# A list of steps per engine in the attention stage, and a whitening without its bias row

## The reference, cut to what matters

```python
x = x + _L0_conv_ref(_ln_c(x), ...)          # windowed attention: 16 heads of 8 channels, windows of 64 tokens
t = t + _L0_ffn_ref(_ln_t(t), ...)           # MoE: softmax of the logits, best 2 of 8 experts, w2(silu(w1 t) * (w3 t))
x = x + _L1_conv_ref(_ln_c(x), gamma, beta)  # whitening in 4 groups of 32 channels
t = t + _L1_ffn_ref(_ln_t(t), ...)           # MoE with biases and a third matrix

def _L1_conv_ref(x, gamma, beta):
    f = jnp.transpose(x, (3, 0, 1, 2)).reshape(C, N)
    mean = jnp.mean(f, axis=1, keepdims=True)
    f = f - mean
    fg = f.reshape(g, m, N)
    cov = jnp.einsum('gmn,gkn->gmk', fg, fg) / (jnp.float32(N) - 1.0)
    ...                                       # sig = cov / trace, three Newton steps for P
    whiten = P / jnp.sqrt(tr)
    fhat = jnp.einsum('gmk,gkn->gmn', whiten, fg)
    return out * gamma + beta
```

## Time and profile before

| | before |
|---|---|
| median of three runs | 790.41 us (789.06 to 793.35) |
| the profiled execution | 785.86 us, span 784.1 us |
| TensorE (PE) busy | 574.4 us, 73% of the span |
| VectorE (DVE) busy | 449.5 us, 57% |
| ScalarE (ACT) busy | 344.2 us, 44% |
| GpSimd (POOL) busy | 424.3 us, 54% |

### The profile page before, as it was taken

The page is one execution under the profiler, slowest core; times in us unless marked ns, Lnnn a source line. Parts: engine busy times, 40 slices in busy tenths (PEclk is TensorE's granted clock), DMA queues, the critical chain, the costliest instruction groups (busy, mean ns, idle before and its releaser), DMA issues. The chain is left out here.

```text
span 784.1 us, 16744 instructions
## 1 busy us (share of the span) xinstructions
PE 574.4 (73%) x5440; PEld 417.1 (53%) x5440; DVE 449.5 (57%) x1248; ACT 344.2 (44%) x860; POOL 424.3 (54%) x417
## 2 busy tenths in 40 slices
PE   3777777876775774869989992997464386999950
PEld 1244454544553563758766671775353265888840
DVE  2675658597684774563434442945662646666635
ACT  2545464453624543656645561431402263555520
POOL 4454345365833464577774445512277774777760
PEclk9858798796966787989979996899866596999985
DMA  9999999999993002231443314200015272556418
GB/s 345 179 177 166 179 160 176 165 168 168 167 166 55 13 29 63 65 104 56 122 133 119 118 60 163 66 2 1 3 45 88 58 123 71 126 132 148 91 40 319
DMA packets 114996, 90.77 MB, mean 116 GB/s; under 512 B 9391, under 2 KB 104760, under 8 KB 114528
## 3 DMA queue, kind: packets, MB, share of 16 engines
q1 hardware_dynamic: 105840, 72.08, 48.8%
q0 software_dynamic: 8640, 16.93, 6.6%
q10 hardware_dynamic: 432, 0.68, 0.3%
HBM read 35.37 MB, written 55.20 MB: 116 GB/s over the span
## 5 line engine op out<-in xcount | busy, mean ns | idle before, releaser
L639 POOL DMA_INDIRECT results<-fetched,rowbuf x142 | 138.0, 972 | 69.9 <-issue 36.1
L940 DVE SCALAR_TENSOR_TENSOR work<-work,rowbuf,bank 128x256 f32<-128x256 f32 x142 | 68.0, 479 | 82.0 <-ACT work L764 67.6
L1314 PE MATMUL bank<-W,work 128*128 x568 | 92.3, 287 | 1.0 <-DVE fetched L947 0.5
L764 ACT ACTIVATE work<-bank 128x256 f32<-128x256 f32 x142 | 54.4, 383 | 78.3 <-PE bank L1301 76.5
L1299 PE MATMUL bank<-Wh,xl 128*128 x142 | 73.1, 515 | 9.6 <-DVE xl L931 6.4
L1314 PEld LDWEIGHTS bank<-W,work 128*128 128x128 f32 x568 | 78.4, 200 | 2.5 <-issue 1.4
L652 POOL DMA_INDIRECT region<-rows_a,where x64 | 63.3, 989 | 22.6 <-issue 19.8
L1306 PE MATMUL bank<-C,work 128*128 128x128 f32 x284 | 57.2, 285 | 17.7 <-DVE work L940 17.6
L1232 PE MATMUL bank<-PT,Vm 64*32 64x64 f32 x2048 | 44.2, 247 | 32.0 <-issue 19.7
L1232 PEld LDWEIGHTS bank<-PT,Vm 64*32 64x32 f32 x2048 | 38.5, 126 | 51.8 <-issue 46.4
L1306 PEld LDWEIGHTS bank<-C,work 128*128 128x128 f32 x284 | 39.9, 146 | 43.0 <-issue 17.4
(11 more groups left out here) (230 smaller groups left out, 1252.7 us busy)
## 6 DMA issues: line engine op xcount, KB each, us to landing
region<-pad SPq DMA_DIRECT2D x32, 1040.0 KB, 19.8
rowbuf<-region SPq DMA_DIRECT2D x142, 65.0 KB
fetched<-results SPq DMA_DIRECT2D x16, 512.0 KB, 4.5
spare<-w1gv_dram SPq DMA_DIRECT2D x8, 640.0 KB
spare<-b_dram SPq DMA_DIRECT2D x71, 64.0 KB
results<-fetched,rowbuf POOLq DMA_INDIRECT x142
work<-w_dram SPq DMA_DIRECT2D x8, 256.0 KB, 12.0
W<-w_dram SPq DMA_DIRECT2D x2, 1024.0 KB, 12.0
```

Of the source, the lines that this page charges most:

```text
L639: pool.indirect_dma_start(results[layer], bass.IndirectOffsetOnAxis(ap=at, axis=0), ysb[:, T % YRING, :], None, bounds_check=PAIRS - 1, oo ...
L764: act.activation(sg[:, i % 2, :], bank[:, b, 0:FF], ACT.Silu).then_inc(sg_sb, 1)
L940: v.scalar_tensor_tensor(out=hh[:, i % 2, :], in0=sg[:, i % 2, :], scalar=tile_rows(i)[:, GATE_AT:GATE_AT + 1], in1=bank[:, b, FF:2 * FF], ...
L1314: last = mm(bank[:, b, 0:P], hT[:, i % 2, ft * P:(ft + 1) * P], W2[layer][:, bass.ds(experts[i] * FT + ft, 1), :].rearrange("p a n -> p (a ...
```

## The change

**The lists.** `LAYER0` becomes a list per engine. A table SHIFT holds, for each engine and kind of step, a number that is added to the step's number before the sort. In `ORDER`, S now stands ahead of O. `MIDDLE` and `LAYER1` are sorted as before.

**The whitening.** `brow`, its product and its sum are gone. ScalarE subtracts the mean from the features (eight activations, which wait for VectorE's value of minus the mean, L1109). GpSimd adds beta to `X` in `MIDDLE`, four steps after a block's c_stats. TensorE waits for the matrix and for a block's centred features; ahead of block 0 it does no warm-up product any more.

```diff
-COV_STEP = {"pair": -1, "sum0": 0, "c_stats": 0, "yc": 1, "yturn": 2, "mean": 2, "cov": 3}
+COV_STEP = {"pair": -1, "sum0": 0, "c_stats": 0, "yc": 1, "yturn": 2, "mean": 2, "cov": 3, "beta": 4}
-ORDER = ("up", "Vm0", "Vm1", "O", "S", "J", "V0", "V1", "ht", "dn", "out", "xt",
+ORDER = ("up", "Vm0", "Vm1", "S", "O", "J", "V0", "V1", "ht", "dn", "out", "xt",
+SHIFT = {
+    "PE": {"T": 0.37, "turn": 0.14, "K": 0.63, "S": -0.35, "J": -0.28, "Q": 0.05, "PT": 0.01, "V1": 0.07, "logits": 0.03},
+    "ACT": {"split": -0.39, "PT": 0.11, "T": 0.44, "exp": 0.97, "turn": 0.27, "rows": 0.17, "Kb1": 0.15, "gates": 1.09, "Vm1": -0.65, "a_y": 0.06},
...
-def in_order(steps):
-    return [(name, i) for _, _, i, name in sorted((s, ORDER.index(name), i, name) for s, name, i in steps)]
+def in_order(steps, shift):
+    return [(name, i) for _, _, i, name in
+            sorted((round(s + shift.get(name, 0), 3), ORDER.index(name), i, name) for s, name, i in steps)]
-LAYER0, MIDDLE, LAYER1 = in_order(first_layer()), in_order(between()), in_order(second_layer())
+LAYER0 = {engine: in_order(first_layer(), SHIFT[engine]) for engine in SHIFT}
+MIDDLE, LAYER1 = in_order(between(), {}), in_order(second_layer(), {})
...
-            if name == "white":
-                if i == 0:
-                    pool.wait_ge(brow_sb, 1)
+            if name == "beta":
                 pool.wait_ge(y_sb["c"], BT * (i + 1))
-                pool.tensor_tensor(xb(i), xb(i), over_tiles(brow[:, :]), ALU.add).then_inc(x_beta, 1)
+                pool.tensor_tensor(xb(i), xb(i), over_tiles(par("beta")), ALU.add).then_inc(x_beta, 1)
...
+            act.wait_ge(newton, MEAN_STEP)
+            for i in range(BLOCKS):
+                wait_freed(act, "yturn", i)
+                act.activation(features(i), features(i), ACT.Identity, bias=minus_mean[:, 0:1]).then_inc(centred, 1)
...
-            dve.wait_ge(newton_ps, 3 * (NEWTON_STEPS - 1) + 4)
-            nc.vector.tensor_tensor(brow[:, :], bank[:, NEWTON1, 0:P], par("beta"), ALU.add).then_inc(brow_sb, 1)
...
                 if i == 0:
-                    pe.wait_ge(brow_sb, 1)
-                warm(b, WARM_BLOCK)
+                    pe.wait_ge(wh_ready, 2)
+                else:
+                    warm(b, WARM_BLOCK)
+                pe.wait_ge(centred, i + 1)
...
-            pe.wait_ge(wh_ready, 2)
-            mm(bank[:, NEWTON1, 0:P], minus_mean[:, 0:1].to_broadcast([P, P]), whiten, start=True, stop=True)\
-                .then_inc(newton_ps, 1)
```

More of the change, by code:

```diff
@@ L134 @@
         3: (18,) * 4 + (19,) * 4 + (20,) * 4 + (21,) * 4}
-ORDER = ("up", "Vm0", "Vm1", "O", "S", "J", "V0", "V1", "ht", "dn", "out", "xt",
+ORDER = ("up", "Vm0", "Vm1", "S", "O", "J", "V0", "V1", "ht", "dn", "out", "xt",
          "a_y", "Kb0", "Kb1", "rows", "route", "white", "max", "sub", "J_add", "stats1", "a_stats", "Q_turn", "K_turn", "sum", "exp",
          "Q0", "Q1", "norm", "yc", "pair", "sum0", "T", "turn", "logits", "gates", "place", "list", "put",
-         "PT", "Q", "K", "split", "fold_w", "fold", "c_stats", "cov", "yturn", "mean")
+         "PT", "Q", "K", "split", "fold_w", "fold", "c_stats", "beta", "cov", "yturn", "mean")
+SHIFT = {
+    "PE": {"T": 0.37, "turn": 0.14, "K": 0.63, "S": -0.35, "J": -0.28, "Q": 0.05, "PT": 0.01, "V1": 0.07, "logits": 0.03},
+    "ACT": {"split": -0.39, "PT": 0.11, "T": 0.44, "exp": 0.97, "turn": 0.27, "rows": 0.17, "Kb1": 0.15, "gates": 1.09, "Vm1": -0.65, "a_y": 0.06},
+    "DVE": {"a_stats": -1.65, "rows": -0.35, "a_y": -1.06, "list": 0.88, "Q_turn": -0.1, "place": 0.45, "max": -0.29, "sum": 0.21},
+    "POOL": {"split": 0.9, "T": 1.49, "route": 0.31, "Q0": -1.38, "K_turn": 0.52, "a_stats": -0.57, "put": -0.3, "Q1": -0.58},
+}
 def tile_steps(layer, at):
@@ L220, in bank_fills @@
     table, needs, filled, turn, pair_end, single_end = {}, {}, [0] * 8, {}, [0] * 8, [0] * 8
-    for name, i in LAYER0 + MIDDLE + LAYER1:
+    for name, i in LAYER0["PE"] + MIDDLE + LAYER1:
         if name in TURNS:
@@ L345, in build @@
         N2, whiten = covd, cov
-        brow = sb("brow", [P, P])
         rowbuf2 = sb("rowbuf2", [P, RING // 2, ROW])
@@ L399, in build @@
         mean_row, means_set = sem("mean_row"), sem("means_set")
-        newton, newton_ps, centre_d, wh_ready, brow_sb = (sem(n) for n in (
-            "newton", "newton_ps", "centre_d", "wh_ready", "brow_sb"))
+        newton, newton_ps, centre_d, wh_ready, centred = (sem(n) for n in (
+            "newton", "newton_ps", "centre_d", "wh_ready", "centred"))
         twin_sb, place_sb = sem("twin_sb"), sem("place_sb")
@@ L412, in build @@
         pair_sum, x_sum, x_beta, stored = sem("pair_sum"), sem("x_sum"), sem("x_beta"), sem("stored")
-        TRACE_STEP, FIRST_STEP = 10, 13
+        MEAN_STEP, TRACE_STEP, FIRST_STEP = 3, 10, 13
         region = [nc.dram_tensor(f"region{l}", (REGION_ROWS, ROW), F32).ap() for l in range(2)]
@@ L672, in _ @@
             pool.wait_ge(ld_const, 32)
-            for name, i in LAYER0:
+            for name, i in LAYER0["POOL"]:
                 pool_step(name, i)
@@ L794, in _ @@
             act.wait_ge(setup, 1)
-            for name, i in LAYER0:
+            for name, i in LAYER0["ACT"]:
                 act_step(name, i)
@@ L1090, in _ @@
             dve.wait_ge(ld_x0, 16)
-            for name, i in LAYER0:
+            for name, i in LAYER0["DVE"]:
                 if (name, i) == ("a_y", 0):
@@ L1110, in _ @@
                                          ALU.mult))
+            assert step[0] == MEAN_STEP
             scale = (1.0 - WHITEN_EPS) / (TOKENS - 1.0)
@@ L1359, in _ @@
             pe.wait_ge(abias_sb, 1)
-            for name, i in LAYER0:
+            for name, i in LAYER0["PE"]:
                 pe_step(name, i)
```

## The result

The changed kernel takes 726.8 us (median of four runs, 723.83 to 728.92) against 789.73; the ratio is 0.9235, 95% interval 0.9148 to 0.9321. The profiled execution took 728.92 us, its span 727.1. The forecast was 748 with 727 to 782. The direction was right. The gain is 63 us where 42 were forecast, and the time lies at the very edge of the range, where case E stood, which had 0.05.

What follows compares the result with a forecast made beforehand. No engine is full in attention, so the chain between engines was taken to bound it. Terms −25 − 9 − 6 + 10.5 − 13.5 = −43 took 785.9 to 742.9, 747.4 at the median; forecast 748 us, range 727 to 782.

Steps and rivals of the forecast that it cites:

- case E: Rival for the whole kernel: more gain, with T1 at −35, T5 at −19.7, T4 at +6, giving 727 us; chance 0.05.
- T1: Attention: scores ahead of O and eviction ahead of exp remove O's waits on TensorE; −25 us, bounds −15 and −35.
- Rival C: Attention: the waits only move, as another link ends last, so T1 gives nothing; 772 us, chance 0.12.
- rival A: Attention: VectorE held at Q_turn between max and sub makes it slower, 812 us; sign: 6 us idle in most blocks; chance 0.08.
- T2: Unit 0's puts one norm earlier end the stall of ScalarE's rows step before unit 2; −9 us, bounds −10 and 0.
- Rival B: Unit 0's puts land only with the zero fills' end, so T2 and about half of T1 go; 769 us, chance 0.10.
- T3: First expert tile: unit 1's last puts, issued earlier, land before TensorE comes; −6 us, bounds −8.7 and 0.
- T4: Tile stage: block 7's power behind twelve more puts holds VectorE and then TensorE; +10.5 us, bounds +6 and +13.
- T5: Layer 1's whitening without the bias row: earlier sums and routing; −13.5 us, bounds −3.3 and −19.7.
- the front: Part of T5, between the whitening matrix and VectorE's first sum: that sum starts 1.9 us earlier.
- routing of unit 6: Part of T5: routing of unit 6 in layer 1 starts at 597.3 instead of 610.59, −13.3 us.
- Two parts costed at nothing: Beta additions (10.2 us) fit GpSimd's idle time in the covariance stage; centring (5 us) hides on ScalarE under the Newton steps.

Runs made afterwards that it cites:

- k1: e3 with both O ahead of the next scores and exp ahead of the eviction again; 729 us, 0.9245 of the kernel before the change.
- e3: The changed kernel with block 7's power back between the fourth and fifth put of unit 2; 720 us, 0.9126 of the kernel before the change.
- h2: k1 with J also behind the O beside it again (J without its shift); 738 us, 0.9348 of the kernel before the change.
- h3: e2 plus block 7's power ahead of the puts and shifts for S, J, exp and PT alone; 754 us, 0.9561 of the kernel before the change.
- e2: The kernel before the change with the new whitening alone, keeping the one old list for attention; 772 us, ratio 0.9787.
- f7: e3 with VectorE's list as before the change (no VectorE shifts); 729 us, 0.9234 of the kernel before the change.
- f4: e3 with O ahead of the next scores again (S without its shift, old ORDER); 719 us, 0.9113 of the kernel before the change.
- f6: e3 with the puts at their old numbers, one norm later; 734 us, 0.9298 of the kernel before the change.
- e8: The changed kernel with the last 8 of layer 1's 17 zero fills issued between loads of tiles 8 to 15; 735 us, 0.9318 of the kernel before.
- g8: e3 with the last 8 of layer 1's 17 zero fills issued one every third tile, 18 to 39; 728 us, 0.9221 of the kernel before.

## Why the prediction was right in sign and 20 us short

*T1, forecast −25, measured −9 for the two moves that it names (k1 against e3, hardly clear) and −18 with J's place (h2 against e3, and h3 against e2).* The step "Removed: at most 31.9 us. What comes in its place ... I take 7 us off" read a wait on TensorE as time of the stage. The waits did go, 23.4 us of them, and the time did not follow one to one. Two things in the traces go with that. With the new lists VectorE is the fullest engine, 34.5 of 36 us in e3's fullest stretch:

```profile
172.00:208.00 36.00, 28.60 (x538) 18.88 (x541) 34.50 (x69) 22.19 (x50) 26.19 (x23) 0.96 1.06 170
```

And what attention gains meets the fills at the first tile, as the table shows. The prediction also called O's the one wait made by the order; VectorE's for J, 30.4 us before, and Q's for the eviction, 23.0, are rows of the engines' waits that it did not read. Which of them sets the time is not shown: 11.7 us of J's wait are back in f7, which its interval does not set apart from e3. Rival C, that the waits only move, is out for the four shifts together (h3) and open for O's waits taken alone (f4); rival A is out by f7 and by VectorE's waits before Q_turn, at most 4.3 us where 6 in most blocks were its sign.

*T2, −9, measured −14 by time (f6, give or take 6), and 7 to 11 where the wait falls.* Right in place, mechanism and size. The wait is the one that was named, 9.12 us before, none after, 8.5 with the puts late. Rival B, that the fills' end holds unit 0's put, is out for this place: in the changed kernel the rows step came 13.4 us after the put and did not wait, while fills went on to be issued until 241 us, and in f6 the puts landed one by one amid the fills. The fills make a put late, but an earlier put does land earlier.

*T3, −6, measured −2 in the changed kernel (8.68 to 6.43) and nothing in e3, where the wait is 11.0.* The step "so they land before TensorE comes to the tile" failed. Unit 1's last puts were issued sooner, as the order said, but 50 us earlier in the run they met the end of the zero fills, and the row loads, which before came 3.2 us behind the put (302.36), came 8.4 behind it. It is rival B's mechanism at the place that the prediction thought free of it. e8 and g8 show that the fills were the cause, since the wait is gone there, and that the fills cannot simply be put into the tile stage.

*T4, +10.5, measured +9 (e3; 9.5 in the traces' first eight tiles).* Right in place, mechanism and size: a wait of 8.54 us where 10.3 were worked out.

*T5, −13.5, measured −17 (e2; in the traces, from the matrix to the end, 17.0 in the changed kernel and 13.4 in e2).* Right: the front gave 1.8 (1.9), routing of unit 6 14.4 (13.3). Two parts costed at nothing, the beta additions and the centring, cost nothing.

*What the sum left out.* The terms as measured make −18 − 14 + 9 − 17 = −40, and the change is worth −60, if the parts simply add. Some 20 us come from shifts that the prediction gave no price: VectorE's list, −8.5 by f7 (not clear of its interval), and about −12 that no run took apart, among them GpSimd's K_turn, Q0, Q1 and T and TensorE's K; of T1's 18, J's 8 had no price either. The step that failed is the silence on them: rival A priced VectorE's new order as a possible loss, and no rival or term had it as a gain. How much of the 20 us is the higher granted clock, 0.876 over the changed kernel's span against 0.833 before, and how much the order itself, stays open: every run with all the new lists shows both. That the time still fell at the range's edge is luck: E put it there with T1 at −35, T4 at +6 and T5 at −19.7, and none of the three came so.

## What to carry to other kernels

Where no engine is full, read the waits of every engine before pricing a reordering, not those of the busiest alone: beside O's wait on TensorE stood J's on VectorE and Q's for the same evictions, and the prediction missed both. Moving work earlier moves it against things with a fixed date, here the zero fills: look up what runs at the new time, and do not take a wait for free because another one behind it hides what it costs. And when a table of numbers moves many steps, check each list's tail by hand for one step that now stands behind a long run of others; taking one such step, the power, back out gave 9 us, and that kernel, at 0.9126 of before, is the one to keep.

## What the runs showed of the hardware

The DMA of a put, 128 rows scattered by GpSimd, landed 2.3 us after its issue in the median of the kernel before, and 8.6 in the median of f6's unit 0, whose puts were all issued amid the fills; in the changed kernel, with fills of 1 MB in flight on SyncE's queue, the load that waited for unit 1's last put came 8.4 us after that put's issue. *The Trainium skill's page "DMA: Bandwidth & Descriptors", section "Queues, rings and completion order", has each DMA engine take turns between the queues it has work for. The trace of f6 agrees so far as this: a put did not wait for all the fills, which went on to be issued until 235 us. What makes a put take 8 us and not 2 beside them, no run here shows.*

VectorE's small operation behind the power, 128 by 4 elements, takes 1.22 us beside GpSimd's addition and 0.16 without; with the beta additions beside it the eight in the covariance stage take 8.9 us instead of 7.5. *By the Trainium skill's page "SBUF — State Buffer", section "SBUF: two separate sides", GpSimd and VectorE share a pair of ports that one of them holds for a whole instruction when both read SBUF. These times agree with it; of the 10 us that it might have cost the traces show 1.4, all of it hidden.*
